# Relu's output brought to the tokens' partitions by VectorE's turned blocks and sixteen transfers inside SBUF

## What is computed

```
xn = layernorm(x)                                  # 32 sequences x 256 tokens x 128
h  = relu(xn @ nm_w1 + nm_b1)                      # "hid"
m  = h @ nm_w2 + nm_b2
q, k, v = m @ q_w + q_b, m @ k_w + k_b, m @ v_w + v_b
att = softmax(q . k / sqrt(128) over the 65 keys around each query) . v
ffn = sum over 16 experts of combine[e] * down_e(silu(gate_e(xn)) * up_e(xn)) + shared expert
out = x + att + ffn                                # combine: top 8 of 16 of a sigmoid router
```

## Time and profile before

| | before |
|---|---|
| time, median of 3 executions | 700.29 us (699.5 to 700.31) |
| profiled execution: its time, its span | 700.29 us, 698.5 us |
| busy share PE, PEld, DVE, ACT, POOL | 98%, 80%, 84%, 63%, 64% |
| chain that ended last | PE 92%, DVE 4%, ACT 2%, issue 1% |
| mean granted clock of PE | 0.996 |
| moved by transfers | 93.94 MB, mean 134 GB/s |

### The profile page before, as it was taken

How to read it: one execution, slowest core, us unless ns; L and a number is a source line. 1 busy time by engine, 2 the same in 40 slices (tenths; PEclk the granted TensorE clock), 3 DMA queues, 4 the chain that set the end, 5 groups by cost and what they waited for, 6 DMA issues and landing times.

```text
span 698.5 us, 10440 instructions
## 1 busy us (share of the span) xinstructions
PE 686.0 (98%) x3232; PEld 560.3 (80%) x3232; DVE 584.9 (84%) x1623; ACT 439.3 (63%) x878; POOL 446.5 (64%) x402
## 2 busy tenths in 40 slices
PE   8899999999999999999999999999999999999997
PEld 5767788888888888888888888888888888888886
DVE  6899997978889787888978889887898978788775
ACT  4775655766656575755766666575755766566573
POOL 4685577666666666677557666666667567665553
PEclk9999999999999999999999999999999999999999
DMA  7716537172562718537182562828447081641800
GB/s 264 196 33 145 160 76 246 45 219 83 125 209 57 234 51 156 173 83 251 34 219 83 128 206 58 230 68 167 145 92 242 33 237 52 153 151 29 230 1 15
DMA packets 84376, 93.94 MB, mean 134 GB/s; under 512 B 8288, under 2 KB 74592, under 8 KB 84320
## 3 DMA queue, kind: packets, MB, share of 16 engines
q1 hardware_dynamic: 84320, 93.28, 47.9%
HBM read 88.49 MB, written 4.77 MB: 134 GB/s over the span
## 4 chain that ended last, share of the span: by engine, by line
PE 92%; DVE 4%; ACT 2%; issue 1%; DVEq 0%
PE ps_u L446 26%; PE ps_y L456 26%; PE ps_g L436 25%; PE bank L374 3%; PE bank L413 3%; PE bank L396 3%; PE ps_y L422 2%; PE bank L403 1%; PE bank L379 1%; PE bank L385 1%; DVE ps_u L1075 1%; PE ps_u L478 1%; DVE h_lo L1081 1%; ACT h_hi L685 1%; ACT prob L666 0%
## 5 line engine op out<-in xcount | busy, mean ns | idle before, releaser
L1181 POOL TENSOR_TENSOR silu_c<-silu,comb_b 128x512 f32<-128x512 f32 x256 | 330.5, 1294 | 233.7 <-ACT silu L677 228.9
L685 ACT ACTIVATE h_hi<-ps_u 128x512 fp32r<-128x512 f32 x272 | 162.7, 598 | 244.9 <-DVE ps_u L1075 244.8
L1081 DVE TENSOR_TENSOR h_lo<-ps_u,h_hi 128x512 fp32r<-128x512 f32 x272 | 186.0, 684 | 47.9 <-ACT h_hi L685 44.3
L1075 DVE TENSOR_TENSOR ps_u<-silu_c,ps_u 128x512 f32<-128x512 f32 x256 | 176.6, 690 | 30.0 <-PE ps_u L446 25.7
L677 ACT ACTIVATE silu<-ps_g 128x512 f32<-128x512 f32 x272 | 162.3, 597 | 0.2
L446 PE MATMUL ps_u<-xn_hi,exp_w_hi 128*128 128x512 f32 x272 | 110.9, 408 | 5.3 <-DVE h_lo L1081 5.2
L456 PE MATMUL ps_y<-h_hi,exp_w_hi 128*128 128x512 f32 x272 | 110.5, 406 | 0.4 <-DVE h_lo L1081 0.4
L436 PE MATMUL ps_g<-xn_hi,exp_w_hi 128*128 128x512 f32 x272 | 108.0, 397 | 0.4 <-ACT silu L677 0.3
L456 PE MATMUL ps_y<-h_lo,exp_w_hi 128*128 128x512 f32 x272 | 107.5, 395 | 0.0
L446 PE MATMUL ps_u<-xn_hi,exp_w_lo 128*128 128x512 f32 x272 | 107.5, 395 | 0.0
L456 PE MATMUL ps_y<-h_hi,exp_w_lo 128*128 128x512 f32 x272 | 107.2, 394 | 0.0
(11 more groups left out here) (153 smaller groups left out, 991.9 us busy)
## 6 DMA issues: line engine op xcount, KB each, us to landing
comb_b<-c_dram SPq DMA_DIRECT2D x63, 1024.0 KB, 12.6
mom_b<-st_dram SPq DMA_DIRECT2D x13, 512.0 KB, 3.8
xin<-x SPq DMA_DIRECT2D x16, 256.0 KB, 3.0
xres<-x_t SPq DMA_DIRECT2D x16, 256.0 KB, 2.7
out_t<-xres SPq DMA_DIRECT2D x16, 256.0 KB, 2.6
xn<-x_t SPq DMA_DIRECT2D x13, 256.0 KB, 3.6
exp_raw<-wexp SPq DMA_DIRECT2D x2, 960.0 KB, 10.3
exp_raw<-wexp SPq DMA_DIRECT2D x1, 768.0 KB, 7.4
```

Of the source, the lines that this page charges most:

```text
L685: A(h_t[hbuf(par, s)][0][:], ps_u[(par + s) % 2][:], ACT.Copy).then_inc(s_h_hi, 1)
L1075: V.tensor_tensor(ps_u[i][:], src[:], ps_u[i][:], ALU.mult).then_inc(s_h, 1)
L1081: V.tensor_tensor(t[1][:], ps_u[(par + s) % 2][:], t[0][:].bitcast(F32), ALU.subtract)\
L1181: G.tensor_tensor(silu_c[i][:].rearrange("p (l x) -> p l x", l=RUNS), silu[i][:].rearrange("p (l x) -> p l x", l=RUNS), comb_b[:, :, s1 - ...
```

## The change

From the second group on, hid is brought to the tokens' partitions in another way. DVE turns the 4x16 blocks of 32x32 elements of hid in one instruction (`hid_blocks`, slot 12), which leaves each block turned but in the wrong partitions; sixteen transfers from SBUF to SBUF (`move_hid`, on SP) put them in their places; ACT `hid_n_hi`, DVE `hid_n_lo` and `key_terms` then read SBUF, not PSUM. Both buffers lie in exp_raw, in space whose weights have been used up, so the first `hid_blocks` waits until all low parts of the weights are made. `hid_relu` moves from slot 13 to 11, `moments` from slot 12 to 15, `variance` from slot 13 to slot 0 of the next group, and SP's part from slot 13 to 12, with chunk 0 ahead of the sixteen transfers and chunks 1 to 3 behind. Group 0 keeps its transposes on PE. PE's `gate` waits for `hid_hi`, no longer for `hn_lo` and `key_term`.

```diff
--- before.py
+++ after.py
@@ -121,6 +121,12 @@
         hid = sb("hid", [P, T])
         hid_t = [sb("hid_hi", [P, T], F32R), sb("hid_lo", [P, T], F32R)]
         q_t = [sb("q_hi", [P, T], F32R), sb("q_lo", [P, T], F32R)]
+        spare = exp_raw[:].rearrange("p s c -> p (s c)")
+        hid_b = spare[:, 3 * T:4 * T].rearrange("p (q c) -> p q c", q=4)
+        hid_m = spare[:, 4 * T:5 * T].rearrange("p (q c) -> p q c", q=4)
         hid_n = [sb("hid_n_hi", [P, TILES, P], F32R), sb("hid_n_lo", [P, TILES, P], F32R)]
         z_t = [sb("z_hi", [P, T], F32R), sb("z_lo", [P, T], F32R)]
         key_prod = sb("key_prod", [P, TILES, P])
@@ -215,11 +221,12 @@
         s_stored = [sem(f"y_stored{i}") for i in range(2)]
 
         names = """bn aggr var_eps rstd mean centred0 centred1 xn xn_tp xn_hi xn_lo gate_mm gate_h gate_s gate_e
-            gate_1 score select top8 rest weight wsum winv comb comb_t
+            hid_b gate_1 score select top8 rest weight wsum winv comb comb_t
             hid_mm hid hid_hi hid_lo q_mm q_hi q_lo hid_tp hn_hi hn_lo key_term
             mask_k sc0 sc1 nmax0 nmax1 exp0 exp1 inv0 inv1 pn0 pn1 pt0 pt1
             p0_hi p0_lo p1_hi p1_lo pv z_hi z_lo""".split()
         S = {n: sem(n) for n in names}
+        s_hid_m = [sem(f"hid_quarter_moved{i}") for i in range(4)]
         s_comb_st = [sem(f"comb_stored{i}") for i in range(2)]
         s_comb_b = [sem(f"comb_b_loaded{i}") for i in range(NCHUNK)]
 
@@ -259,6 +266,12 @@
             return b[:, 0:2 * APART].rearrange("p (t c) -> p t c", t=2)[:, :, 0:WIN]
 
         gate_raw = att_raw[:, GATE:GATE + E].rearrange("p (o e) -> p o e", o=1).to_broadcast([P, 4, E])
+        moved = hid_m.rearrange("p q (a f) -> p a q f", f=32)
+        def quarters(t):
+            return t.rearrange("p a (q f) -> p a q f", q=4)
 
         @block.sync
         def _(sp):
@@ -307,6 +320,18 @@
                              c_dram[par].rearrange("(o l e) x -> o l (e x)", o=1, l=RUNS)
                              [:, :, c * CHUNK * T // RUNS:(c + 1) * CHUNK * T // RUNS]
                              .to_broadcast([P, RUNS, CHUNK * T // RUNS])).then_inc(s_comb_b[c], 16)
+            def move_hid(g):
+                sp.wait_ge(S["hid_b"], g)
+                if g > 1:
+                    sp.wait_ge(S["hn_lo"], g)
+                    sp.wait_ge(S["key_term"], 2 * g)
+                for q in range(4):
+                    for t in range(4):
+                        sp.dma_start(hid_m[t * 32:(t + 1) * 32, q, :], hid_b[q * 32:(q + 1) * 32, t, :])\
+                            .then_inc(s_hid_m[q], 16)
 
             def prologue():
                 load_x(0, 0)
@@ -353,9 +378,11 @@
                         load_x(g + 3, 1 - par)
                     if TURNED <= g + 2 < GROUPS:
                         spread_moments(g + 2)
-                if s == 13 and not last(g):
+                if s == 12 and not last(g):
                     store_comb(g + 1, 1 - par)
-                    for c in range(NCHUNK):
+                    spread(g + 1, 1 - par, 0, False)
+                    move_hid(g + 1)
+                    for c in range(1, NCHUNK):
                         spread(g + 1, 1 - par, c, False)
 
             def finish():
@@ -467,9 +494,9 @@
                 pe.wait_ge(S["hid_lo"], g + 1)
                 project(bank[1], 1, hid_t).then_inc(S["q_mm"], 1)
 
-            def hid_turn(g):
-                pe.wait_ge(S["hid_lo"], g + 1)
+            def hid_turn():
+                pe.wait_ge(S["hid_lo"], 1)
                 turn(bank[0], hid).then_inc(S["hid_tp"], 1)
 
             def spin(times):
@@ -509,7 +536,7 @@
                     pe.wait_ge(s_fresh, 2)
                     fresh_weights(3, bank[2])
                 if s == 3:
-                    hid_turn(0)
+                    hid_turn()
 
                     pe.wait_ge(s_scw, 1)
                     pe.wait_ge(s_row, 1)
@@ -569,15 +596,15 @@
                 if s == when(g, 4, 7) and more:
                     pe.wait_ge(S["xn_lo"], g + 2)
 
-                    pe.wait_ge(S["hn_lo"], g + 1)
-                    pe.wait_ge(S["key_term"], 2 * g + 2)
+                    pe.wait_ge(S["hid_hi"], g + 1)
+                    if first(g):
+                        pe.wait_ge(S["hn_lo"], 1)
+                        pe.wait_ge(S["key_term"], 2)
                     gate(1 - par)
                 if s == when(g, 5, 7):
                     scores(1)
                 if s == 15 and more:
                     q_proj(g + 1)
-                if s == 16 and more:
-                    hid_turn(g + 1)
 
             def att_late(g, par, s):
 
@@ -652,8 +679,15 @@
                 A(q_t[0][:], bank[1][:], ACT.Identity, bias=vecs[:, 7:8]).then_inc(S["q_hi"], 1)
 
             def hid_n_hi(g):
-                act.wait_ge(S["hid_tp"], g + 1)
-                A(flat(hid_n[0]), bank[0][:], ACT.Copy).then_inc(S["hn_hi"], 1)
+                if first(g):
+                    act.wait_ge(S["hid_tp"], 1)
+                    A(flat(hid_n[0]), bank[0][:], ACT.Copy).then_inc(S["hn_hi"], 1)
+                else:
+                    act.wait_ge(S["pv"], g)
+                    for q in range(4):
+                        act.wait_ge(s_hid_m[q], 64 * g)
+                    A(quarters(hid_n[0][:]), moved, ACT.Copy).then_inc(S["hn_hi"], 1)
 
             def z_hi(g):
                 act.wait_ge(S["pv"], g + 1)
@@ -752,7 +786,7 @@
                     prob_hi(g, 0)
                 if s == when(g, 9, 12):
                     prob_hi(g, 1)
-                if s == 13 and more:
+                if s == 11 and more:
                     hid_relu(g + 1)
                 if s == 15:
                     z_hi(g)
@@ -897,19 +931,41 @@
                                        in1=q_t[0][:].bitcast(F32), op0=ALU.add, op1=ALU.subtract)\
                     .then_inc(S["q_lo"], 1)
 
+            def hid_blocks(g):
+                dve.wait_ge(S["hid"], g + 1)
+                if g == 1:
+                    dve.wait_ge(s_expw, STEPS - len(DVE_LO))
+                    dve.wait_ge(s_expw_late, len(DVE_LO))
+                if g > 1:
+                    for q in range(4):
+                        dve.wait_ge(s_hid_m[q], 64 * (g - 1))
+                V.transpose(hid_b.rearrange("p q c -> p (q c)"),
+                            hid[:].rearrange("p (a q t) -> p q a t", a=TILES, q=4)).then_inc(S["hid_b"], 1)
             def hid_n_lo(g):
                 dve.wait_ge(S["hn_hi"], g + 1)
-                V.tensor_tensor(flat(hid_n[1]), bank[0][:], flat(hid_n[0]).bitcast(F32), ALU.subtract)\
-                    .then_inc(S["hn_lo"], 1)
+                if first(g):
+                    V.tensor_tensor(flat(hid_n[1]), bank[0][:], flat(hid_n[0]).bitcast(F32), ALU.subtract)\
+                        .then_inc(S["hn_lo"], 1)
+                else:
+                    V.tensor_tensor(quarters(hid_n[1][:]), moved, quarters(hid_n[0][:]).bitcast(F32),
+                                    ALU.subtract).then_inc(S["hn_lo"], 1)
 
             def key_terms(g, seq):
 
                 if first(g) and seq == 0:
                     dve.wait_ge(s_row, 1)
                     dve.wait_ge(s_vec2, 1)
+                for q in range(4):
+                    if not first(g):
+                        dve.wait_ge(s_hid_m[q], 64 * g)
                 for a in range(2 * seq, 2 * seq + 2):
+                    tile = bank[0][:, a * P:(a + 1) * P].rearrange("p (q f) -> p q f", q=4) if first(g) \
+                        else moved[:, a, :, :]
                     done = V.tensor_tensor_reduce(
-                        out=key_prod[:, a, :], in0=bank[0][:, a * P:(a + 1) * P], in1=key_row[:], scale=1.0,
+                        out=quarters(key_prod[:])[:, a, :, :], in0=tile,
+                        in1=key_row[:].rearrange("p (q f) -> p q f", q=4), scale=1.0,
                         scalar=vecs[:, 6:7], op0=ALU.mult, op1=ALU.add, accum_out=key_term[:, a:a + 1])
                 done.then_inc(S["key_term"], 1)
 
@@ -1031,13 +1087,14 @@
                         moments(g + 2, par)
                     if s == 5:
                         variance(g + 2)
-                if s == 12 and TURNED < g + 3 < GROUPS:
+                if s == 0 and TURNED < g + 2 < GROUPS:
+                    variance(g + 2)
+                if s == 12 and more:
+                    hid_blocks(g + 1)
+                if s == 13 and first(g):
+                    moments(g + 2, par)
+                if s == 15 and TURNED < g + 3 < GROUPS:
                     moments(g + 3, 1 - par)
-                if s == 13:
-                    if first(g):
-                        moments(g + 2, par)
-                    elif g + 3 < GROUPS:
-                        variance(g + 3)
                 if s == 14:
                     if first(g):
                         variance(g + 2)
```

## The result

The kernel before took 700.13 us (median, 699.47 to 700.31, 5 executions), the changed one 707.08 us (704.66 to 708.62, 5 executions). The ratio is 1.0097, with a 95% interval of 1.0081 to 1.0114: slower by 6.95 us, where I had forecast 3.7 us faster. The profiled execution of the changed kernel took 705.2 us, its span is 703.4 us.

What follows compares the result with a forecast made beforehand. The prediction took the kernel as PE-bound from 85 to 664 us, with thin margin in slots 7 to 12. It summed 700.29 - 6.60 + 2.6 + 0.3 = 696.6 us, range 693.8 to 701.0.

Steps and rivals of the forecast that it cites:

- PE's transposes: On PE, 15 groups lose their four transposes of hid at 0.44 us each group: 6.60 us saved.
- order moves: Relu in slot 11, `moments` in slot 15 and `variance` in slot 0 fit into existing cover: cost nothing.
- DVE's turn: On DVE, the 128x512 turn takes 0.7 us, at most 791 ns, in the old place of `moments`: cost nothing.
- pause in group 0: The first turn waits for POOL's 15th low part, so PE's `up_proj` of slot 13 starts late: +2.6 us.
- rival B: PE's clock falls after the new pause in group 0, 1.7 us lost, time 698.3 us; chance 0.15.
- two inputs in SBUF: `hid_n_lo` and `key_terms` reading SBUF collide with POOL; group 1 pays 0 to 0.6 us, taken as 0.3.
- sixteen transfers: On SP's queue from 433.5, 6.9 us of issues, landed by 443 to 444, before ACT needs them: nobody waits.
- ACT's and DVE's cover in slots 11 to 15: ACT's idle 1.02 us hides relu in slot 11; later slots' gaps of 1.8 us and more hide DVE's moved work.
- In number of pieces the small one is the nearer, so I take 0.43: Issue time of each small transfer on SP, taken at 0.43 us between bounds 0.43 and 1.07: 6.9 us for sixteen.
- Hidden, by 1 to 3 us: Transfers land by 443 to 444, ahead of ACT's `hid_n_hi` at 444.76, which has 1.20 us idle behind it.
- rival E: Transfers come late for ACT once issues take 0.68 us each; at 1.07, about 790 us; chance 0.07.
- Rival D: POOL's `mask_k` pair beats `xn_lo` once that comes over 1.15 us late: 6.3 us over 14 groups, 702.9; chance 0.13.

Runs made afterwards that it cites:

- experiment 2: The kernel before with only the order moves (relu, moments, variance, SP's part); no turn on DVE, no transfers: 700.21 us.
- experiment 8: The changed kernel with one 128x512 transfer replacing the sixteen, and DVE's first turn waiting for only 6 and 1 low parts; output differs: 694.01 us.
- 4: The changed kernel with one transfer of 128x512 in place of the sixteen, same bytes, same queue place; output differs: 698.19 us.
- experiment 5: The changed kernel with chunk 0 of the routing weights cut from 1 MB to 128 KB ahead of the sixteen transfers; output differs: 698.20 us.
- Experiment 3: The changed kernel without the sixteen transfers, ACT and DVE reading the turned blocks where they lie; output differs: 698.24 us.
- experiment 7: The changed kernel with four more 16 KB transfers to an unused place, twenty in all, which `hid_n_hi` also waits for: 743.07 us.
- experiment 1: The changed kernel with DVE's first turn waiting for 6 low parts of POOL and 1 of DVE, not 15 and 2: 704.79 us.
- experiment 6: The changed kernel with the looser first wait, the sixteen replaced by one DRAM store behind chunk 0 and four loads: 700.29 us.
- experiment 9: The changed kernel with the looser first wait, the sixteen replaced by a DRAM store ahead of chunk 0 and four loads after it: 695.18 us.

## Why the prediction was wrong, step by step

| term | predicted, us | measured, us |
|---|---|---|
| PE's transposes | -6.6 | about -6.35 (0.42 in each of 15 groups) |
| order moves | 0 | 0 (experiment 2) |
| DVE's turn | 0.7 long, 0 on the path | 0.705 long, 0 |
| pause in group 0 | +2.6 | +2.5 |
| clock behind it (rival B) | 0 in the forecast, 1.7 in B | +1.7 |
| two inputs in SBUF | +0.3 | about 0.15, with all the rest (experiment 8) |
| sixteen transfers | 0 | +8.9 (707.08 - 698.19) |

The way from the kernel before to the changed one is 700.22 - 6.21 (experiment 8) + 4.18 (from 8 to 4) + 8.89 (from 4 to the changed kernel) = 707.08. That it adds up proves nothing, since each term is the difference of two runs. What supports the terms is what the traces show of each: 0.42 us a group, a pause of 2.5 us with 1.7 us of clock, and the waits for transfers. The last term is the least certain. Between the two profiled executions it is 7.2 us (705.2 against 697.98), and the two slowest executions of the changed kernel, 708.43 and 708.62 us, had a mean clock of 0.994 and 0.992 against 0.998 in the two fastest, so a part of the 8.9 is probably clock lost behind the late transfers.

- **Right:** the price of the transposes, within 0.02 us a group; the turn, by the slope from the earlier trace rows (all 15 lie between 703 and 711 ns); ACT's and DVE's cover in slots 11 to 15; and the wait in group 0, with the engine, the place and nearly the size, 2.48 us against 2.6.
- **The step that failed** is "In number of pieces the small one is the nearer, so I take 0.43", with its end "Hidden, by 1 to 3 us". A transfer of 16 KB from SBUF to SBUF takes 0.59 us of SP's queue, and the sixteen together 10.0 to 11.1 us with little ahead of them in the DMA engines, 11.0 to 13.4 behind chunk 0, where I had 6.9. The landing of 2.4 us came from a row with nothing issued in the 11 us ahead of it; behind chunk 0 the median is 3.7 and the most 9.2 us. An issue 0.16 us longer than taken looks like nothing, but it is multiplied by 16 and uses up the 1 to 3 us of cover. By itself that still costs no time (experiment 5); with the longer issues and landing behind chunk 0 it does.
- **My own point of decision** in rival E, 0.68 us for each, was good: in group 9 of experiment 5, with 10.87 us (0.68), ACT doesn't wait, in that of the changed kernel, with 13.35 us (0.83), it waits 2.64 us. What was wrong was a chance of 0.07 for it. The two bounds were 0.43 and 1.07, the point stood between them, and I had no row that said on which side.
- **Rival B came true.** The clock is at its lower level of 1.2 GHz for a while after the pause. It was so in each of the four other profiled kernels that kept the pause in slot 13 (experiments 3, 4, 5 and 7) and in none of the five that had it removed. I gave it 0.15, because the shorter pause of 1.31 us had not done it. The price, 1.7 us, was right, but the earlier trace rows, from which I took it, shows clock lost and not time lost: the profiled execution of the changed kernel has no fall at 24 us, and PE idles there instead (3.69 of 4 us busy). That of experiment 2 has none either and takes the time of before, 700.31 against 700.29 us:

```profile
24.00:28.00 4.00, 3.68 (x19) 2.85 (x18) 3.35 (x6) 4.00 (x10) 2.38 (x3) 1.00 0.74 214
```

In that stretch PE waits for DVE anyway, and a low clock costs nothing. After 58 us it costs all.

- **Rival D did not happen**, not even where DVE was late enough. Group 10 of the changed kernel, with the longest wait for transfers, DVE and POOL, against the earlier trace rows:

```profile
457.79 0.69 DVE L860 TENSOR_TENSOR xn_lo<-xn,xn_hi 128x512 fp32r<-128x512 f32 x1
...
457.72 1.89 POOL L1219 TENSOR_SCALAR mask_k<-mask,key_term 128x160 f32<-128x160 f32 x2
```

Counted from the group's first expert `gate`, `xn_lo` comes 2.1 us later than before, past the 1.15 us at which D was to decide. But `mask_k` comes 2.1 us later too, which D had not allowed for, and the two meet as before: `xn_lo` takes its 0.69 us, and it is POOL's pair that takes 1.89 us. Experiment 3 has the same reads and all its groups from 2 on at 41.35 us, so nothing is lost here.

The Trainium skill's page DMA: Bandwidth & Descriptors says under "Issuing engines are not separate DMA queues" that the sequencer's time to start a transfer is "usually small relative to the DMA itself". Here it isn't, 0.59 us against 1.8 us of landing, and since issues don't overlap and landings do, issue is what adds up. The same page's rule against transfers below 64 KB, which I had let pass, pointed the right way. Its fixed cost (about 2.0 us, which it gives under "Anatomy of one DMA" for transfers issued by GpSimd, not SP) sixteen times over, an estimated 32 us, would have been two and a half times the 11 + 1.8 us that were measured in experiment 5.

What stays open: why a few of the issues behind chunk 0 take 1.0 to 2.3 us. Without most of that chunk the sixteen take 10.0 to 11.1 us and no issue over 1.55, so what lies ahead bears on them; by which mechanism no run here tells. Open too is what decides whether a pause of PE of about 2 us is followed by the lower clock. And no run issues a part of the sixteen from another engine's queue, so whether SP's 11 us can be shared isn't shown.

## What to carry to other kernels

A transfer has two prices, its issue on a queue that does one thing at a time and its landing behind what lies ahead. Count issues first, put the transfer whose landing is awaited ahead of the bulk that nobody awaits yet, and ask who needs the bulk that you push back. If the point at which a rival decides lies between your two bounds, the forecast isn't the better half but a toss, and the chances should say so. When two costs follow each other, removing one shows less than its price (some 2.3 us in experiment 1, 4.2 us between 4 and 8).

## What the runs showed of the hardware

- SP's issue time: 0.59 us (median) for 16 KB from SBUF to SBUF over 32 partitions, 0.53 us for 256 KB over 128 partitions. So it hardly follows the bytes. It also depends on what lies ahead: the 256 KB store to DRAM took 0.32 us ahead of chunk 0 and 0.52 us behind it, the four loads of 64 KB from DRAM 0.43 us each in experiment 6 (1.74 for four) and 0.98 us each right behind chunk 0 in experiment 9 (3.92 for four).
- The same 256 KB store to DRAM lands after 2.2 us ahead of a 1 MB transfer and after 9.3 us behind it.
- The pause of PE of 2.5 us in slot 13 of group 0 was followed by 1.7 us lost to the lower clock in all five profiled kernels that had it, and so was one of 1.77 us in experiment 1. One of 1.15 us, at 454.72 in the changed kernel, was not. The length alone doesn't decide: in experiment 7 pauses of 2.0 to 2.9 us were followed by it and one of 2.20 us was not, and the pause of 2.12 us near 23 us was followed by it in the profiled execution of the kernel before and not in that of the changed one.
- A turn of 128x512 on DVE takes 0.705 us, about as long as any 128x512 operation there.
